# A two-layer graph network on one core: the sums of a group of edges scattered one group behind the gathers' turn instead of two

## The chip, the cores and the metric

The kernel runs on 1 core of one Trainium2 chip. What is measured is the device time of one execution in microseconds; the kernel before takes 5044.54 us, the median of 3 runs (5033.79 to 5050.71).

## The reference

A graph of 50,000 nodes with 256 features and 50,000 edges, sorted by `dst`, goes through two layers, each with a residual and a layer norm:

```
x = layernorm(x + GAT(x, src, dst, edge_attr_32))       # attention, 4 heads of 64
h = concat(x[src], x[dst])                              # 50000 x 512
h = tanh(h @ W0 + b0); h = tanh(h @ W1 + b1); h = h @ W2 + b2
h = h * (edge_attr_128 @ Wg)
out = layernorm(x + segment_mean(h, src, n))
```

Everything is float32. The change is in the second layer, the edge network: for each edge, two rows of a table are gathered and added, a small network runs on them, and the result is added to the row of `out` that `src` names.

## The kernel before, in words

The kernel is a row of stages, each a block in which all engines run their own program. The edge network is the block that begins at L1493; the stage before it has already written, for each node, the rows of two tables in the chip's memory: PA (the part of `x @ W0` for one end of an edge, with the reciprocal of the node's number of edges in column F0) and PB (that for the other end), and has put `x` into `out`. The stage after it reads `out` and normalizes it.

**Tiling.** Edges are worked on in 98 groups (`GROUPS`) of 4 tiles (`G`) of 128 edges. Buffers are double, by the parity `s` of the group `g`; a "turn" is one pass of each engine's `body(g, ...)`. `late(g, n)` and `early(g, n)` leave work out in the last and first n turns. There is no planner: each engine's order is written out by hand, and semaphores tie the engines together. `need(engine, sem, n)` is a wait, left out if n is not positive.

**GpSimd** issues all indirect DMAs of the stage, strictly in its order. `gather(s, j)` (L1508 to L1513) issues two, a tile's rows of PA into `u_pa` and of PB into `u_pb`; the two have one line, L1510. `free(g)` waits until the buffers of a group may be written: the adds of the group two before it (`v_sum`) and its transposes (`p_t`) must be done. `scatter(g, s, j)` (L1521 to L1531, DMA at L1528) adds the 128 rows of sums of tile j from `u_sums` to the rows of `out` named in `u_row`. It waits for ScalarE's copy of the sums (`a_y`, one copy for j = 0, 1 and one for j = 2, 3), for VectorE's row numbers (`v_si`), and for j = 0 and 2 until all scatters issued before have landed (`o_st`). Before the loop, groups 0 and 1 are gathered. In turn g GpSimd calls `free(g + 2)`, then gathers tiles 0, 1 of group g + 2, scatters two tiles, gathers tiles 2, 3, scatters two tiles (L1538 to L1547).

**VectorE** in turn g selects for group g - 1 (`select`: which edges have the same `src`), computes its row numbers (`scatter_rows`, L1805), subtracts for the low parts of layers 1 and 2 (`low0(g + 1)`, `low1(g)`), multiplies by the gate (`message(g, j)`, L1810), and late in the turn adds the gathered rows of group g + 2: `add_first` (L1747), which waits until all eight gathers of the group have landed, then `message(g, 3)`, then `add_rest`. The order there is message 2, low part of 1, add_first, message 3, low parts of 2 and 3, add_rest; the select of group g follows at the start of the next turn.

**TensorE** in turn g: layer 1 of group g in three parts (nine products at L1580 and one at L1594 each), between which stand the transposes of group g + 1 (L1568, part k needs the k-th add); then `combine(g - 1, 0)` (L1620, adds up messages with the same `src` within a tile or a pair of tiles), the gate and layer 2 of group g, with the transposes of edge features and `combine(g - 1, 1)` between.

**ScalarE** does the tanh's in the same order, and `sums(g - 1, 0)` and `sums(g - 1, 1)` (L1696), which copy the combined messages of group g - 1 to `u_sums` in turn g. The first waits until the scatters of group g - 3 have landed.

**SP** loads edge features and keys, and waits for transposes and selections only.

Of the kernel before, what the change touches and what calls it, by code (L numbers as in the profile page):

```python
# [22 lines left out]
G = 4  # L23
# [33 lines left out]
def gnn_kernel(nc, x, src, dst, e128, e32, lin_W, att_src, att_dst, lin_edge_W, att_edge, bias,  # L57
# [7 lines left out]
    GROUPS = N // (G * P) + 1  # L65
# [36 lines left out]
    def groups(eng, body):  # L102


        for g in range(GROUPS):
            body(g, g % 2, g // 2, g == GROUPS - 1)
# [17 lines left out]
    def need(eng, sem, n):  # L124

        if not (isinstance(n, int) and n <= 0):
            eng.wait_ge(sem, n)

    def early(g, n):

        return isinstance(g, int) and g < n

    def late(g, n):

        return isinstance(g, int) and g + n >= GROUPS
# [11 lines left out]
    with top:  # L147
# [1314 lines left out]
        with ph:  # L1462
# [26 lines left out]
                                                        sem("u_msg_low"), sem("u_selected"), sem("u_scatter_rows"))  # L1489
            TB, LB, QB, CB = (B[0], B[1]), (B[2], B[3], B[4]), (B[5], B[6]), B[7]  # L1490
            NK = [n for _, n in M0[:3]] + [T0]

            with nc.Block() as block:  # L1493
# [12 lines left out]
                @block.gpsimd  # L1506
                def _(pool):
                    def gather(s, j):  # L1508
                        for q, (buf, table, w) in enumerate(((pa, PA, AW), (pb, PB, F0))):
                            pool.indirect_dma_start(  # L1510
                                out=buf[s][:, j, 0:w], out_offset=None, in_=table,
                                in_offset=bass.IndirectOffsetOnAxis(ap=ix[s][:, 1 - q, j:j + 1], axis=0))\
                                .then_inc(gath[s], 16)  # L1513

                    def free(g):
                        pool.wait_ge(v_ix, g + 1)
                        need(pool, v_sum, 4 * (g - 1))
                        need(pool, p_t, 4 * (g - 1))
                        pool.sem_inc(turn, 1)

                    def scatter(g, s, j):  # L1521

                        pool.wait_ge(a_y, 2 * g + j // 2 + 1)
                        pool.wait_ge(v_si, g + 1)
                        if j % 2 == 0:
                            need(pool, o_st, 16 * (4 * g + j))
                        pool.sem_inc(turn, 1)
                        pool.indirect_dma_start(  # L1528
                            out=out, out_offset=bass.IndirectOffsetOnAxis(ap=si[s][:, j:j + 1], axis=0),
                            in_=yo[s][:, j, :], in_offset=None, bounds_check=N - 1, oob_is_err=False,  # L1530
                            compute_op=ALU.add).then_inc(o_st, 16)  # L1531

                    for g in range(2):
                        free(g)
                        for j in range(G):
                            gather(g, j)

                    def body(g, s, i, last):  # L1538
                        if not late(g, 2):
                            free(g + 2)  # L1540
                        for h in range(G // 2):
                            for j in (2 * h, 2 * h + 1):
                                if not late(g, 2):
                                    gather(s, j)
                            for j in (2 * h, 2 * h + 1):
                                if not early(g, 2):
                                    scatter(g - 2, s, j)  # L1547
                    groups(pool, body)
                    for g in range(GROUPS - 2, GROUPS):
                        for j in range(G):  # L1550
                            scatter(g, g % 2, j)
                    pool.wait_ge(o_st, 16 * G * GROUPS)

                @block.tensor
                def _(pe):
# [45 lines left out]
                    def layer2(g, s, j):  # L1601
                        e = slice(j * P, (j + 1) * P)
                        for k, (_, n) in enumerate(M1):
                            n += k == 2
                            if j == 0:
                                pe.wait_ge(v_hm, 3 * g + k + 1)
                            o = product(QB[j % 2][:, 0:D], [h2[q][0:n, k, e] for q in range(2)],
                                        [w2r[q][0:n, k, :] for q in range(2)], k == 0, k == 2)
                        o.then_inc(p_q, 1)
# [368 lines left out]
```

## Time and profile before

| | |
|---|---|
| median of the runs | 5044.54 us |
| span of the profiled execution | 5498.8 us |
| edge network in it, first gather to last scatter | 3303.8 to 5183.7 us |
| TensorE matmul busy, whole span | 4252.2 us, 77% |
| VectorE, ScalarE, GpSimd busy | 3806.6, 3248.7, 3300.0 us |
| indirect DMAs of the edge network | 784 gathers, 392 scatters |

The runs were timed without the profiler, and the times in the rows are of another execution, with it. Of that one only the span, from its first to its last instruction, is given and no time of its own on the runs' scale; it is 454 us longer than the median. Times in rows are microseconds from the span's start. On GpSimd a DMA's duration is what the engine spends on issuing it, not the transfer. A matmul's end is modelled, and some records can be missing.

### The profile page before, as it was taken

The numbers are of one execution on the slowest core, as the hardware profiler recorded it, in microseconds if no ns is written. First come the engines' busy times: TensorE is split into PE (matmuls) and PEld (weight loads), VectorE is DVE, ScalarE is ACT, GpSimd is POOL, SyncE is SP. The second block draws the span as 40 slices with busy tenths as digits, with TensorE's granted clock in tenths as the row PEclk, the third lists the DMA queues.
The fourth block names the chain that finished last, engine by engine and source line by source line (L and its number), as shares of the span: only waits on it lengthen the run. The fifth ranks groups of instructions, "written<-read, shape, count | busy, mean of one in ns | idle before, by whom it ended". The sixth has DMA issues, their size and how long they took to land. (4 is left out here: it accounts for less than half of the span.)

```text
span 5498.8 us, 87081 instructions
## 1 busy us (share of the span) xinstructions
PE 4252.2 (77%) x24476; PEld 3420.0 (62%) x24476; DVE 3806.6 (69%) x12195; ACT 3248.7 (59%) x7255; POOL 3300.0 (60%) x3036
## 2 busy tenths in 40 slices
PE   6777777777657776599999997889989999999500
PEld 3455545555434444599999995777777777777400
DVE  7766666666656665798989875666666666666564
ACT  7755555555533343366666665666666676666575
POOL 0255555555666665455555546777777888888532
PEclk9999999999977887799999998999999999999755
DMA  3232322323275555699999995666666666666596
GB/s 82 55 86 80 87 80 81 88 80 84 71 150 166 166 165 166 221 368 354 367 353 365 355 322 139 143 141 145 144 150 139 146 149 148 147 151 145 144 394 275
DMA packets 774331, 975.10 MB, mean 177 GB/s; under 512 B 182069, under 2 KB 685148, under 8 KB 761084
## 3 DMA queue, kind: packets, MB, share of 16 engines
q0 software_dynamic: 170176, 323.19, 26.3%
q10 hardware_dynamic: 269085, 374.19, 18.9%
q1 hardware_dynamic: 334715, 273.49, 16.5%
q8 instruction: 162, 2.65, 0.2%
q14 instruction: 193, 1.58, 0.1%
HBM read 541.99 MB, written 429.16 MB: 177 GB/s over the span
## 5 line engine op out<-in xcount | busy, mean ns | idle before, releaser
L1381 PE MATMUL bank<-w0r,n_x1T 128*128 128x406 f32 x4704 | 905.8, 352 | 36.1 <-issue 16.9
L1381 PEld LDWEIGHTS bank<-w0r,n_x1T 128*128 128x128 f32 x4704 | 870.4, 190 | 59.9 <-ACT n_pa L1429 35.3
L1528 POOL DMA_INDIRECT out_x<-u_sums,u_row x392 | 639.5, 1631 | 143.8 <-issue 116.8
L580 POOL DMA_INDIRECT DS<-by_dst,rank_int x392 | 376.0, 959 | 572.8 <-DVE rank_int L750 427.8
L1580 PE MATMUL bank<-u_h,w1r 128*108 128x512 f32 (+1 forms) x2646 | 680.0, 401 | 0.0
L406 PEld LDWEIGHTS bank<-wst,xT 128*128 128x128 f32 x2352 | 332.2, 201 | 430.1 <-issue 311.4
L406 PE MATMUL bank<-wst,xT 128*128 128x264 f32 x2352 | 409.5, 312 | 242.6 <-DVE xps L415 196.8
L832 POOL DMA_INDIRECT xg<-XP,m_src x392 | 420.3, 1072 | 222.7 <-DVE msg L892 113.5
L1257 POOL DMA_INDIRECT n_cg<-CT,n_last x392 | 445.8, 1137 | 175.3 <-issue 95.2
L1510 POOL DMA_INDIRECT u_pa<-PA,u_rows x392 | 408.5, 1042 | 202.1 <-issue 111.1
L1580 PEld LDWEIGHTS bank<-u_h,w1r 128*108 128x108 f32 (+1 forms) x2646 | 436.6, 172 | 127.1
L1580 PE MATMUL bank<-w2r,u_h 108*128 108x256 f32 x3528 | 486.0, 282 | 7.0 <-DVE u_h L1775 6.9
L586 POOL DMA_INDIRECT DS<-r_s_dst,r_head_rows x392 | 387.9, 990 | 142.1 <-issue 117.3
L1510 POOL DMA_INDIRECT u_pb<-PB,u_rows x392 | 396.8, 1012 | 120.6 <-issue 117.9
L1684 ACT ACTIVATE u_gate<-bank,u_rc 128x256 f32<-128x256 f32 x392 | 186.6, 476 | 462.0 <-PE bank L1580 251.8
L1580 PEld LDWEIGHTS bank<-w2r,u_h 108*128 108x128 f32 x3528 | 448.6, 190 | 9.1 <-DVE u_h L1775 8.5
L1810 DVE TENSOR_TENSOR u_message<-bank,u_gate 128x256 f32<-128x256 f32 x392 | 166.1, 424 | 382.6 <-ACT u_gate L1684 262.0
L663 PE MATMUL bank<-table,ohloT 128*128 128x392 f32 x784 | 349.4, 529 | 44.5 <-ACT ohloT L603 43.5
L1568 PE MATMUL bank<-ident,u_pb 128*128 128x128 f32 (+1 forms) x1568 | 246.3, 280 | 157.6 <-DVE u_pb L1747 60.5
L1568 PEld LDWEIGHTS bank<-ident,u_pb 128*128 128x128 f32 (+1 forms) x1568 | 172.8, 137 | 266.9 <-issue 163.9
L718 DVE CUSTOM_DVE_ANT_0 found<-bank,onehot,earlier 128x392 f32<-128x392 f32 x392 | 243.0, 620 | 132.9 <-PE bank L663 58.7
L415 DVE TENSOR_TENSOR xps<-bank,biasx 128x264 f32<-128x264 f32 x392 | 166.0, 423 | 242.9 <-remote 232.7
(286 smaller groups left out, 10637.8 us busy)
## 6 DMA issues: line engine op xcount, KB each, us to landing
PA<-n_pa ACTq DMA_DIRECT2D x98, 816.0 KB
PB<-n_pb ACTq DMA_DIRECT2D x98, 812.0 KB
XP<-xps ACTq DMA_DIRECT2D x98, 528.0 KB
CT<-ct ACTq DMA_DIRECT2D x98, 528.0 KB
n_xp<-XP SPq DMA_DIRECT2D x98, 528.0 KB
xin<-in_x SPq DMA_DIRECT2D x97, 512.0 KB
n_x<-in_x SPq DMA_DIRECT2D x97, 512.0 KB
out_x<-n_x ACTq DMA_DIRECT2D x97, 512.0 KB, 4.8
```

The lines of the kernel that those rows point to most:

```text
L406: o = nc.tensor.matmul(acc[:, 0:XW], xT[k][p][:, h, j * P:(j + 1) * P], wst[q][:, h, :], start=(n == 0), stop=(n == 5))
L580: pool.indirect_dma_start(out=DS, out_offset=bass.IndirectOffsetOnAxis(ap=ri[s][:, j:j + 1], axis=0), in_=pd[s][:, j, :], in_offset=None). ...
L586: pool.indirect_dma_start(out=DS, out_offset=bass.IndirectOffsetOnAxis(ap=hx[s][:, j:j + 1], axis=0), element_offset=8, in_=sn[s][:, j, :] ...
L663: nc.tensor.matmul(UB[j % 2][:, 0:NT], oT[s][:, j * P:(j + 1) * P], tab[s][:], start=True, stop=True)\
L718: nc.vector.tensor_tensor_reduce(out=lkj[j % 2][:], in0=UB[j % 2][:, 0:NT], in1=ohhi[0][s][:, j, :], scale=1.0, scalar=cnt[s][:, j:j + 1], ...
L832: pool.indirect_dma_start(out=xg[r][:, j, :], out_offset=None, in_=XP, in_offset=bass.IndirectOffsetOnAxis(ap=sr[r][:, j:j + 1], axis=0))\
L1257: pool.indirect_dma_start(out=cg[s][:, j, :], out_offset=None, in_=CT, in_offset=bass.IndirectOffsetOnAxis(ap=il[s][:, j:j + 1], axis=0)). ...
L1381: o = nc.tensor.matmul(acc, xT[s][p][:, k, e], w0r[q][:, 2 * half + k, :], start=(n == 0), stop=(n == len(terms) - 1))
L1510: pool.indirect_dma_start(out=buf[s][:, j, 0:w], out_offset=None, in_=table, in_offset=bass.IndirectOffsetOnAxis(ap=ix[s][:, 1 - q, j:j + ...
L1528: pool.indirect_dma_start(out=out, out_offset=bass.IndirectOffsetOnAxis(ap=si[s][:, j:j + 1], axis=0), in_=yo[s][:, j, :], in_offset=None, ...
L1568: o = nc.tensor.transpose(TB[k % 2][0:n, j * P:(j + 1) * P], pb[s][:, j, a:a + n], ident[:])
L1580: o = nc.tensor.matmul(acc, a[p], b[q], start=(start and n == 0), stop=(stop and n == 2))
```

## The change

In GpSimd's loop, the scatters of turn g are those of group g - 1, whose parity is 1 - s, instead of those of group g - 2. They start in turn 1 instead of turn 2, and behind the loop one group is left to scatter instead of two. The other engines' programs are the same, and so are the numbers of DMAs and their sizes.

```diff
                             for j in (2 * h, 2 * h + 1):
-                                if not early(g, 2):
-                                    scatter(g - 2, s, j)
+                                if not early(g, 1):
+                                    scatter(g - 1, 1 - s, j)
                     groups(pool, body)
-                    for g in range(GROUPS - 2, GROUPS):
-                        for j in range(G):
-                            scatter(g, g % 2, j)
+                    for j in range(G):
+                        scatter(GROUPS - 1, 1, j)
                     pool.wait_ge(o_st, 16 * G * GROUPS)
```

## Rows read from the trace of the kernel before

**Rows 1.** Costliest groups of the page: busy us, mean ns | idle before, its main releaser.
```profile
L1528 POOL DMA_INDIRECT out_x<-u_sums,u_row x392 | 639.5, 1631 | 143.8 <-issue 116.8
```
**Rows 2.** Windows, turns 2 to 96: length, busy time of each engine, clock, DMA.
```profile
core 0: us, PE busy (x) PEld busy (x) DVE busy (x) ACT busy (x) POOL busy (x), PEclk, DMA share, GB/s
3374.28:5135.69 1761.41, 1606.02 (x10342) 1346.51 (x10340) 1158.91 (x3107) 1201.90 (x2353) 1384.76 (x1124) 0.99 0.66 145
```
**Rows 3.** Timeline, TensorE (start, length): marks of turns 2, 49 and 96.
```profile
3374.28 0.40 PE L1594 MATMUL bank<-u_h1t,w1t 86*108 86x512 f32 x1
...
4268.95 0.40 PE L1594 MATMUL bank<-u_h1t,w1t 86*108 86x512 f32 x1
...
5135.69 0.40 PE L1594 MATMUL bank<-u_h1t,w1t 86*108 86x512 f32 x1
```
**Rows 4.** Waits of GpSimd, edge network: total us, times, longest.
```profile
POOL u_pa L1510 <- PE bank L1568: 57.0, 23, 10.0
...
POOL out_x L1528 <- DMA out_x<-u_sums,u_row: 23.5, 7, 4.2
...
POOL out_x L1528 <- ACT u_sums L1696: 3.2, 1, 3.2
```
**Rows 5.** Timeline, GpSimd, one turn: first gather, second scatter pair, next turn's gathers.
```profile
4501.74 1.02 POOL L1510 DMA_INDIRECT u_pa<-PA,u_rows  x1 [0.32 <-issue]
...
4516.46 1.62 POOL L1528 DMA_INDIRECT out_x<-u_sums,u_row  x1 [0.30 <-issue]
...
4520.28 1.02 POOL L1510 DMA_INDIRECT u_pa<-PA,u_rows  x1 [0.31 <-issue]
...
4524.14 0.95 POOL L1510 DMA_INDIRECT u_pb<-PB,u_rows  x1 [0.30 <-issue]
```
**Rows 6.** Timeline, ScalarE, same turn: copies of the sums.
```profile
4500.23 0.68 ACT L1696 COPY u_sums<-bank 128x512 f32<-128x512 f32 x1
...
4504.07 0.58 ACT L1696 COPY u_sums<-bank 128x512 f32<-128x512 f32 x1
...
4517.82 0.68 ACT L1696 COPY u_sums<-bank 128x512 f32<-128x512 f32 x1
```
**Rows 7.** Timeline, VectorE, same turn: first add, then message 3.
```profile
4506.49 0.68 DVE L1747 TENSOR_TENSOR u_pb<-u_pb,u_pa 128x512 f32<-128x512 f32 x1
4510.20 0.42 DVE L1810 TENSOR_TENSOR u_message<-bank,u_gate 128x256 f32<-128x256 f32 x1 [3.03 <-ACT u_gate L1684]
```
**Rows 8.** Timeline, TensorE, same turn: transposes and layer 1.
```profile
4508.66 0.60 PE L1568 MATMUL bank<-ident,u_pb 128*128 128x128 f32 x4
...
4509.02 2.33 PE L1580 MATMUL bank<-u_h,w1r 128*108 128x512 f32 x9
...
4512.19 0.66 PE L1568 MATMUL bank<-ident,u_pb 128*128 128x128 f32 x4 [0.60 <-DVE u_pb L1747]
```
**Rows 9.** Timeline, start of the stage: eighth gather, VectorE's first add.
```profile
3312.69 0.95 POOL L1510 DMA_INDIRECT u_pb<-PB,u_rows  x1 [0.30 <-issue]
...
3315.93 1.89 DVE L1747 TENSOR_TENSOR u_pb<-u_pb,u_pa 128x512 f32<-128x512 f32 x3 [10.74 <-DMA u_pb<-PB,u_rows]
```
**Rows 10.** Timeline, end of the stage: sums of group 96, scatters.
```profile
5158.32 0.60 ACT L1696 COPY u_sums<-bank 128x512 f32<-128x512 f32 x1
...
5160.36 1.55 POOL L1528 DMA_INDIRECT out_x<-u_sums,u_row  x1 [3.22 <-DMA out_x<-u_sums,u_row]
...
5182.10 1.55 POOL L1528 DMA_INDIRECT out_x<-u_sums,u_row  x1 [0.30 <-issue]
```
**Rows 11.** Windows: turn 5, and a part of it.
```profile
3430.34:3451.73 21.39, 18.68 (x112) 15.93 (x113) 13.37 (x36) 13.73 (x28) 16.33 (x15) 0.92 0.67 138
...
3442.50:3445.80 3.30, 3.01 (x14) 3.04 (x15) 1.85 (x4) 2.00 (x4) 2.39 (x4) 0.50 0.59 170
```
**Rows 12.** Timeline, TensorE: two waits, and matmuls behind the first.
```profile
3358.68 0.66 PE L1568 MATMUL bank<-ident,u_pb 128*128 128x128 f32 x4 [2.40 <-DVE u_pb L1747]
...
3359.10 2.34 PE L1580 MATMUL bank<-u_h,w1r 128*107 128x512 f32 x9
...
3441.55 0.62 PE L1580 MATMUL bank<-w2r,u_h 108*128 108x256 f32 x3 [1.28 <-DVE u_h L1775]
```

## The prediction

> **What bounds the kernel now.** I read the page first for where GpSimd stands, then the windows of the edge network, then single turns of its loop. A turn is the time in which the kernel's bodies work on one group of 512 edges; there are 98. The change touches only GpSimd's order of indirect DMAs in this stage.
>
> One row has all the full turns: from turn 2 to turn 96, TensorE is busy 1606 of 1761 us (91%) and GpSimd 1385 (79%), at a granted clock of 0.99 [rows 2]. The last layer-1 matmul of a turn's first third marks its start; by the first and last of these marks 94 turns take 1761.41 us, 18.74 each; from turn 49 on 47 turns take 866.74 us, 18.44 each [rows 3].
>
> GpSimd is fuller than 79%. In one turn its first gather starts at 4501.74 and that of the next turn at 4520.28: 18.54 us, filled by 8 gathers and 4 scatters with 0.30 us before each [rows 5]. Its real waits in the whole stage are 57.0 us for transposes (23 times), and 3.2 us once for the sums that a scatter reads [rows 4]. So GpSimd and TensorE both need about 18.4 us a turn, and GpSimd stays in step because what it does in a turn was ready long before: the gathers run two groups ahead, the scatters take sums made one turn earlier.
>
> **The change, part by part.** In turn g GpSimd issues: gathers j=0,1 of group g+2; two scatters; gathers j=2,3; two scatters. Number, order and size of the DMAs stay. The four scatters are now those of group g-1, not g-2. What is removed is a turn of slack; what is added is that the first pair waits for ScalarE's first copy of the sums of g-1, which is made in this same turn.
>
> Queued behind that wait are the four gathers j=2,3 of group g+2 and the other pair. VectorE's first add of g+2 wants all eight gathers and stands in VectorE's queue before message(g,3), so the late gathers hold VectorE, then TensorE (the transposes of g+2 after its first third of layer 1, and the combination of group g), and so the next copy of sums. It is a closed loop of one turn:
>
> 1. Copy done, GpSimd sees it: 0.30 us, the idle that stands before each of its DMAs [rows 5].
> 2. Two scatters and four gathers: from 4516.46 to 4524.14 + 0.95 = 4525.09, so 8.63 us [rows 5].
> 3. From the last gather's end on GpSimd to its landing. At the start of the stage the eighth gather ends at 3312.69 + 0.95 = 3313.64 and VectorE, waiting for it, starts at 3315.93: 2.29 us [rows 9]. It is an almost empty queue there, so this is a lower end; I take 2.3 and allow 3.
> 4. The first add: 0.68 us [rows 7].
> 5. From there to the next copy's end. VectorE starts message(g,3) at 4510.20 and the copy ends at 4517.82 + 0.68 = 4518.50: 8.30 us, the lower end [rows 6, 7]. By TensorE: transposes 0.60, layer 1's second third from 4509.02 to the next transposes at 4512.19, less their wait of 0.60, 2.57 us, then from 4512.19 to 4518.50, 6.31 us: with 0.1 of hand-over 9.6 us, the upper end [rows 6, 8]. I take 9.0, since the two chains cross: ScalarE's activations need TensorE's products and the reverse.
>
> Sum: 0.30 + 8.63 + 2.3 + 0.68 + 9.0 = 20.9 us (20.2 to 22.2), against 18.74 now. GpSimd's own work of 18.5 fits inside it.
>
> The check from the other side: today message(g,3) starts 4510.20 - 4500.91 = 9.29 us after the copy ended [rows 6, 7]. After the change the gathers land 11.2 us after it and the add ends at 11.9. That is 2.6 us late, and what fills the 9.29 us today (the rest of layer 2, the next layer 1) can all be done within the 11.9. This turn, 9.29 + 8.30 = 17.6 us, is shorter than the mean; on the mean, 2.6 us more would be 21.3, between the ends.
>
> The second pair of scatters costs nothing: the second copy starts 3.84 us after the first, while GpSimd still has 8.63 us to do [rows 5, 6]. Nor does the wait of each pair for the landing of the pair before: four gathers lie between, as now. SP's loads are tied to transposes and selections, not to scatters.
>
> **The clock.** TensorE will have a gap of 2 to 3 us in each turn, between its layer-1 third and the late transposes. In the trace such a gap is at times followed by the lower level, 1.2 GHz: behind a 1.28 us wait at 3441.55 the clock reads 0.50 for 3442.50 to 3445.80, and that turn took 21.39 us at a mean of 0.92 [rows 11, 12]. But behind the gap of 2.40 us at 3358.68 nine layer-1 matmuls took 2.34 us, as long as the 2.33 of nine at 4509.02 [rows 8, 12]. Lost by such an episode is 8% of 21.39, 1.7 us of matmuls, and it would lie on the path, just behind the gap. I take one turn in two: 0.85, so 21.7 us. The Trainium skill ("TensorE: Matmul & The Clock Gate", Part 1: The HAM clock gate) says that the clock is binary, half rate as the default after idleness and full rate only after sustained work. By that rule each turn could pay, and the sum would be 22.6 us a turn and not 21.7; the rows so far show both outcomes.
>
> **Ends.** Turns 1 to 95 have gathers behind the wait: 95 turns. At the end, the sums of group 96 are ready at 5158.92; today's last four pairs start at 5160.36, some 6.6 us apart, because each waits for the pair before to land, and end at 5183.65. With the change four pairs are left too, of groups 96 and 97, and the first starts at 5159.2: 1.1 us gained [rows 10].
>
> Total: 95 x (21.7 - 18.74) = 281, less 1: +280 us. The profiled execution spans 5498.8 us, so its successor about 5779. That span is 454 us above the median of 5044.5 of the runs timed; the page doesn't say where. I carry the difference over as it is, 5325, or in proportion (5.1%), 5301, and say 5320.
>
> **The rivals.**
> - *The clock falls in every turn.* 20.9 + 1.7 = 22.6 us, 95 x 3.86 = 367, so 5410. For it: the gap is there in every turn. Against: the 2.40 us gap. Chance 0.18.
> - *The runs without a profile have a shorter loop.* If the 454 us lie in the 2352 indirect DMAs (six groups of 392 on the page; one is in [rows 1]), each is 0.19 us shorter, the six in the loop 1.2 us. With the clock's share it is 20.5 against 18.74: +170, so 5215. Chance 0.15.
> - *No change.* The loop is shorter than a turn of today, so the wait costs nothing. All of 20.9 - 18.7 = 2.2 us would have to go, 0.37 us of each of the six DMAs, over a third of a gather's 0.95. Chance 0.04.
> - *Faster.* Turns 2 to 48, in which GpSimd is early and waits for transposes, take 894.67 us, 19.04 each; from 49 on, where it runs later, 18.44 [rows 3, 4]. If its early gathers disturb TensorE's feeders, tying GpSimd to this turn's sums gives all turns the later phase: 47 x 0.60 = 28 us, so 5016. The point from which this decides is whether the gathers land before their add is due: it must start 9.29 - 0.68 = 8.6 us after the copy, and they land at 11.2. 2.6 us are missing, each turn. Chance 0.04.
> - *The scatters don't really move*, because something else holds them. Their rows (v_si) and sums are made in the turn in which they now stand, and the landing of the previous pair came in time in all but 7 cases, 23.5 us [rows 4]. I see nothing that could; it has no chance of its own.
>
> **How the numbers follow.** The forecast, 5320, has 0.59; its own range is 5230 (20.9 us a turn and no clock loss gives 205 us, so 5249, or 188 less in proportion, 5232) to 5400. The range of 8 in 10 goes from 5190, which takes in most of the shorter loop, to 5430. A measurement of this kernel can tell about 0.3% (15 us) from no change. Slower by more: 0.59 + 0.18 + 0.15 = 0.92; within: 0.04; faster: 0.04.
>
> **What would show it in the profile after.** GpSimd's busy time stays near 3300 us, but before the scatters there is idle time ended by ScalarE's copy of the sums, about 3 us in each of some 95 turns, 250 to 350 us, where it is 3.2 now [rows 4]. The last gather of a turn ends some 9 us behind the copy. VectorE waits before the first add for the landing of the gathers, 4 to 6 us a turn, and TensorE before the transposes of L1568 for VectorE, 2 to 3 us a turn. The marks stand 21 to 22.5 us apart. The clock in the edge network shows dips beside 0.99: in half of the turns if I am right on that term.
>
> I am wrong if the marks stay within 19 us (then the gathers weren't late, or VectorE's add had more slack than 9.29 us shows), or if GpSimd's wait for the sums is long but VectorE's for the gathers is not.

## The result, and the profile after

The kernel after takes 5597.91 us (median of 4 runs, 5593.02 to 5601.06) beside 5039.16 us for the kernel before: 1.1096 times as long, 95% interval 1.1078 to 1.1115. Run again, on a chip where the kernel before takes 5049.11 us, it takes 5605.28 us, 1.1103 (1.1086 to 1.1120). I had forecast 5320 us: the right side and the right mechanism, but 280 us of a loss of 559, and 5598 lies outside my range of 8 in 10 (5190 to 5430).

A chip turned up later on which the kernel before takes 5525 us, where the others take some 5040 to 5050. Two other kernels were profiled on it, and they reach the first gather of the edge network at 3324 and 3348 us; the first profile of the kernel before (5498.8 us) reaches it at 3304, every other profile at 2917 to 2936. So the first profile most likely comes from a chip of that slower kind; which one it was isn't recorded, and the kernel before was not profiled there again. A second profile of the unchanged kernel, which spans 5051.9 us, is therefore what the kernel after is compared with here.

The page of the kernel after, in the columns of [rows 1]; the lines are those of L1528 and L1747, now L1746.

```profile
L1528 POOL DMA_INDIRECT out_x<-u_sums,u_row x392 | 645.1, 1646 | 706.9 <-ACT u_sums L1695 604.7
...
L1746 DVE TENSOR_TENSOR u_pb<-u_pb,u_pa 128x512 f32<-128x512 f32 x294 | 198.7, 703 | 617.3 <-DMA u_pb<-PB,u_rows 617.3
```

GpSimd's busy time is as before, but ahead of the scatters it now waits 604.7 us for ScalarE's copy of the sums, where [rows 4] had 3.2; VectorE waits 617.3 us for gathers, 6.3 us a turn.

The marks of turns 2 and 96 as in [rows 3], then windows as in [rows 2] of the same 94 turns, of three parts of turn 62, and of the whole stretch in it at the lower level, before and behind the start of its transposes:

```profile
2984.80 0.40 PE L1593 MATMUL bank<-u_h1t,w1t 86*108 86x512 f32 x1
...
5227.77 0.40 PE L1593 MATMUL bank<-u_h1t,w1t 86*108 86x512 f32 x1
```

```profile
core 0: us, PE busy (x) PEld busy (x) DVE busy (x) ACT busy (x) POOL busy (x), PEclk, DMA share, GB/s
2984.80:5227.77 2242.97, 1808.05 (x10341) 1519.58 (x10340) 1176.34 (x3101) 1201.46 (x2350) 1352.18 (x1129) 0.86 0.52 115
4413.00:4419.00 6.00, 2.79 (x15) 1.85 (x13) 0.37 (x2) 0.77 (x2) 4.78 (x5) 1.00 0.65 156
4419.50:4426.00 6.50, 5.53 (x16) 4.16 (x17) 6.21 (x20) 2.81 (x6) 5.09 (x5) 0.50 0.65 111
4426.50:4431.80 5.30, 5.30 (x38) 4.62 (x37) 2.59 (x5) 4.65 (x10) 0.00 (x0) 1.00 0.48 163
...
4419.41:4420.47 1.06, 0.00 (x0) 0.00 (x0) 0.82 (x2) 0.00 (x0) 0.78 (x1) 0.50 0.57 48
4420.47:4426.24 5.77, 5.77 (x17) 4.40 (x18) 5.59 (x20) 3.05 (x6) 4.55 (x5) 0.50 0.64 119
```

A turn takes 2242.97 / 94 = 23.86 us. The clock is 0.86 in the mean, because within each of the 94 turns it reads 1.00, then 0.50, then 1.00 again; in this one it is at 0.50 for 6.83 us, from 4419.41 to 4426.24. Here is that turn's loop, from one copy of sums to the next; it answers to [rows 5 to 8]. Timeline of the kernel after, by engine:

```profile
4407.29 0.62 ACT L1695 COPY u_sums<-bank 128x512 f32<-128x512 f32 x1
...
4431.23 0.62 ACT L1695 COPY u_sums<-bank 128x512 f32<-128x512 f32 x1
```

```profile
4408.84 1.62 POOL L1528 DMA_INDIRECT out_x<-u_sums,u_row  x1 [5.83 <-ACT u_sums L1695]
...
4412.65 1.02 POOL L1510 DMA_INDIRECT u_pa<-PA,u_rows  x1 [0.30 <-issue]
...
4416.51 0.95 POOL L1510 DMA_INDIRECT u_pb<-PB,u_rows  x1 [0.30 <-issue]
...
4432.78 1.62 POOL L1528 DMA_INDIRECT out_x<-u_sums,u_row  x1 [6.41 <-ACT u_sums L1695]
```

```profile
4419.65 0.77 DVE L1746 TENSOR_TENSOR u_pb<-u_pb,u_pa 128x512 f32<-128x512 f32 x1 [6.28 <-DMA u_pb<-PB,u_rows]
4420.34 0.41 DVE L1809 TENSOR_TENSOR u_message<-bank,u_gate 128x256 f32<-128x256 f32 x1
```

```profile
4415.40 0.40 PE L1593 MATMUL bank<-u_h1t,w1t 86*108 86x512 f32 x1
...
4420.47 1.11 PE L1567 MATMUL bank<-ident,u_pb 128*128 128x128 f32 x4 [4.68 <-DVE u_pb L1746]
...
4421.24 4.19 PE L1579 MATMUL bank<-u_h,w1r 128*108 128x512 f32 x9
```

The copy ends at 4407.91; the scatter starts at 4408.84, the last gather ends at 4417.46, the add starts at 4419.65, and the next copy ends at 4431.85. TensorE has been idle for 4.68 us when the transposes come, and the nine layer-1 matmuls behind them take 4.19 us where nine took 2.33 in [rows 8]: the clock granted to them is the lower level, 1.2 GHz.

The same rows of the kernel before in its second profile: the windows of turns 2 to 96, and one turn.

```profile
2997.95:4682.31 1684.36, 1570.78 (x10341) 1338.41 (x10340) 1160.48 (x3097) 1201.86 (x2349) 1342.67 (x1122) 0.99 0.70 152
```

```profile
3846.50 1.02 POOL L1510 DMA_INDIRECT u_pa<-PA,u_rows  x1 [0.30 <-issue]
...
3864.34 1.02 POOL L1510 DMA_INDIRECT u_pa<-PA,u_rows  x1 [0.31 <-issue]
```

```profile
3853.53 0.74 DVE L1747 TENSOR_TENSOR u_pb<-u_pb,u_pa 128x512 f32<-128x512 f32 x1 [2.59 <-DMA u_pb<-PB,u_rows]
...
3854.32 0.66 PE L1568 MATMUL bank<-ident,u_pb 128*128 128x128 f32 x4 [0.94 <-DVE u_pb L1747]
```

A turn takes 1684.36 / 94 = 17.92 us there, not 18.74. GpSimd has no idle time but its 0.3 us, and VectorE already waits 2.59 us for its gathers: GpSimd bounds the kernel before on these chips. The difference of 5.94 us over 95 turns is 564 us, beside the measured 559.

### The profile page after: what moved, and what is told of

It is laid out like the page before. It is cut to its first block and busy times, and to the rows that moved or that the text cites. A ratio compares the mean times of both kernels' runs of the same rounds, so it can differ in the third digit from the quotient of the medians.

```text
span 5595.5 us, 87081 instructions
## 1 busy us (share of the span) xinstructions
PE 4335.8 (77%) x24476; PEld 3537.5 (63%) x24476; DVE 3832.6 (68%) x12195; ACT 3247.0 (58%) x7255; POOL 3263.0 (58%) x3036
## 5 line engine op out<-in xcount | busy, mean ns | idle before, releaser
L1528 POOL DMA_INDIRECT out_x<-u_sums,u_row x392 | 645.1, 1646 | 706.9 <-ACT u_sums L1695 604.7
L1579 PE MATMUL bank<-u_h,w1r 128*108 128x512 f32 (+1 forms) x2646 | 854.8, 479 | 0.0
L1567 PE MATMUL bank<-ident,u_pb 128*128 128x128 f32 (+1 forms) x1568 | 311.5, 335 | 471.8 <-DVE u_pb L1746 461.3
L1579 PEld LDWEIGHTS bank<-u_h,w1r 128*108 128x108 f32 (+1 forms) x2646 | 543.3, 213 | 172.2
L1746 DVE TENSOR_TENSOR u_pb<-u_pb,u_pa 128x512 f32<-128x512 f32 x294 | 198.7, 703 | 617.3 <-DMA u_pb<-PB,u_rows 617.3
L1567 PEld LDWEIGHTS bank<-ident,u_pb 128*128 128x128 f32 (+1 forms) x1568 | 244.6, 174 | 562.7 <-DVE u_pb L1746 483.3
L1689 ACT CAST u_msg<-u_message 128x256 fp32r<-128x256 f32 x392 | 158.4, 404 | 614.3 <-DVE u_message L1809 614.3
L406 PE MATMUL bank<-wst,xT 128*128 128x264 f32 x2352 | 384.1, 299 | 116.8 <-DVE xps L415 111.8
L1672 ACT ACTIVATE u_h<-bank,b1s 108x512 fp32r<-108x512 f32 (+1 forms) x294 | 201.9, 687 | 293.4 <-PE bank L1593 293.4
L1774 DVE TENSOR_TENSOR u_h<-bank,u_h 108x512 fp32r<-108x512 f32 (+1 forms) x294 | 202.4, 688 | 198.0 <-ACT bank L1673 198.0
L663 PE MATMUL bank<-table,ohloT 128*128 128x392 f32 x784 | 322.6, 493 | 0.0
```

The source lines that it names most:

```text
L406: o = nc.tensor.matmul(acc[:, 0:XW], xT[k][p][:, h, j * P:(j + 1) * P], wst[q][:, h, :], start=(n == 0), stop=(n == 5))
L663: nc.tensor.matmul(UB[j % 2][:, 0:NT], oT[s][:, j * P:(j + 1) * P], tab[s][:], start=True, stop=True)\
L1528: pool.indirect_dma_start(out=out, out_offset=bass.IndirectOffsetOnAxis(ap=si[s][:, j:j + 1], axis=0), in_=yo[s][:, j, :], in_offset=None, ...
L1567: o = nc.tensor.transpose(TB[k % 2][0:n, j * P:(j + 1) * P], pb[s][:, j, a:a + n], ident[:])
L1579: o = nc.tensor.matmul(acc, a[p], b[q], start=(start and n == 0), stop=(stop and n == 2))
L1774: nc.vector.tensor_tensor(h2[1][0:n, m, :], LB[m][0:n, :], h2[0][0:n, m, :].bitcast(f32), ALU.subtract).then_inc(v_hm, 1)
```

## The experiments

Each was timed beside the kernel before on the same chip; `turn` is the mean of turns 2 to 96 in its profile.

| kernel | us | beside before | ratio (95%) | turn | clock |
|---|---|---|---|---|---|
| before again | 5050.35 | 5050.35 | 0.9997 (0.9985 to 1.0009) | 17.92 | 0.99 |
| after | 5597.91 | 5039.16 | 1.1096 (1.1078 to 1.1115) | 23.86 | 0.86 |
| after, filled | 5371.80 | 5050.35 | 1.0639 (1.0618 to 1.0660) | 21.26 | 1.00 |
| one slot | 5051.39 | 5050.35 | 0.9999 (0.9986 to 1.0012) | 17.98 | 1.00 |
| three and one | 5230.31 | 5050.35 | 1.0353 (1.0332 to 1.0374) | 19.96 | 0.93 |
| three and one, filled | 5124.61 | 5048.27 | 1.0147 (1.0128 to 1.0165) | 18.87 | 1.00 |
| four first | 5325.73 | 5048.27 | 1.0549 (1.0531 to 1.0567) | 20.91 | 0.91 |
| before, three scatters | 4887.25 | 5048.27 | 0.9681 (0.9665 to 0.9698) | 16.39 | 1.00 |
| after, add later | 5603.33 | 5048.27 | 1.1096 (1.1073 to 1.1119) | 23.89 | 0.86 |
| one and three, other chip | 6185.92 | 5524.98 | 1.1205 (1.1140 to 1.1270) | 25.63 | 0.83 |
| before, filled, other chip | 5555.50 | 5524.98 | 1.0058 (1.0024 to 1.0091) | 19.30 | 0.98 |
| before, filled | 5056.25 | 5049.11 | 1.0014 (1.0005 to 1.0023) | 18.01 | 1.00 |

**The kernel before again.**

> The kernel before, unchanged, for a second profile of it. The first profile spans 5498.8 us where its timed runs take 5039, the profile of the kernel after 5595.5 where they take 5598. If the first profile was an unusual execution, this one spans about 5040 us, its edge network has turns of about 18.0 us (5598 - 5039 = 559 us over 95 turns is 5.9, and the changed kernel's turns are 23.89), and the stages before the edge network are as long as in the changed kernel (2920 us to its first gather). If profiling lengthens this kernel alone, it spans about 5500 again. Time: same as before.

It spans 5051.9 us, so profiling does not lengthen this kernel: the profiled execution took 5053.66 us and the nine others 5038.5 to 5058.6. The rows above of the kernel before are from this run.

**The clock alone: the kernel after, with its gap filled.** Twelve matmuls, whose result the transposes overwrite.

```diff
+                    def fill(g, s, n):
+                        need(pe, v_e, g + 1)
+                        for _ in range(n):
+                            nc.tensor.matmul(TB[0][0:108, :], w1r[0][:, 0, 0:108],
+                                             h1[s][0][:, 0, :], start=True, stop=True)
...
                         layer1(g, s, 0)
                         if ahead:
+                            fill(g, s, 12)
                             transposes(g + 1, 1 - s, 0)
```

> The kernel after, with 12 extra 512-column matmuls of TensorE in each turn (their result is overwritten) in the gap before the transposes that wait for the late gathers. They need about 3 us and stand in a gap of 4.7 us. Theory A (a closed loop of 21 us a turn through the late gathers, and on top the clock, which falls in every turn behind the gap and costs 2 to 3 us): the clock of the edge network returns to 0.97 to 1.0, the turn shrinks from 23.9 to 21 to 21.5 us, the time to 5320 to 5380 us; the wait for the gathers stays. Theory B (the clock is a companion, the turn is set by GpSimd's and the DMA queue's order alone): the clock returns but the turn stays at 23.9 us or grows, 5600 us or more.

Windows of turns 2 to 96, and TensorE around the gap (the filler is L1573), in the filled kernel:

```profile
3007.62:5006.00 1998.38, 1823.37 (x11470) 1523.90 (x11468) 1158.36 (x3101) 1199.83 (x2350) 1343.60 (x1129) 1.00 0.60 129
```

```profile
4368.81 2.91 PE L1573 MATMUL bank<-u_h,w1r 128*108 128x512 f32 x12
4373.37 0.66 PE L1567 MATMUL bank<-ident,u_pb 128*128 128x128 f32 x4 [1.66 <-DVE u_pb L1752]
4373.78 2.33 PE L1584 MATMUL bank<-u_h,w1r 128*108 128x512 f32 x9
```

TensorE does 2.91 us more work a turn and still waits 1.66 us for the add, the nine matmuls are back at 2.33 us, and the turn is 2.60 us shorter. So the time splits as theory A has it: 21.26 us of loop, 2.60 us of clock. Theory B is out. The parts of the loop say where the 2.60 us lie. In the mean of 92 turns of the timelines, from the end of a copy to the end of the last gather it is 9.56 us in both kernels, from there to the end of the add 2.92 unfilled and 2.96 filled, and from the add to the end of the next copy 11.41 us unfilled and 8.74 filled. Only the last part, in which TensorE's chain runs, has changed.

**One slot earlier instead of two.** The loop, against the kernel before; behind it six tiles are left to scatter.

```diff
-                            for j in (2 * h, 2 * h + 1):
-                                if not early(g, 2):
-                                    scatter(g - 2, s, j)
+                            for j in (0, 1):
+                                if h == 0 and not early(g, 2):
+                                    scatter(g - 2, s, 2 + j)
+                                if h == 1 and not early(g, 1):
+                                    scatter(g - 1, 1 - s, j)
```

> Half of the change: the scatters come one pair of slots earlier than before, not two (in turn g first tiles 2, 3 of group g-2, then, behind all gathers of g+2, tiles 0, 1 of group g-1). GpSimd still waits for sums made in the same turn, but no gather of group g+2 stands behind that wait. Theory A: the loop is open, the gathers land some 15 us before they are due, turns of 18 us, 5040 us within 1%. Theory B' (waiting for sums of the same turn is what costs, whatever stands behind it): half or more of the loss, 5300 us or more.

No difference. It is a weaker test than I meant: GpSimd is late enough in these turns that it waited for the sums in only 2 places (11.3 us). What it shows is that a pair taken from the same turn's sums costs nothing in this place, where the sums are nearly always ready and no gather of g+2 stands behind it. What a real wait would cost there was not tested.

**Half of the gathers behind the wait.**

```diff
-                            for j in (2 * h, 2 * h + 1):
+                            for j in ((0, 1, 2), (3,))[h]:
                                 if not late(g, 2):
                                     gather(s, j)
```

> The kernel after, but three tiles of group g+2 are gathered before the first pair of scatters and one behind it, so two gather DMAs stand behind the wait and not four. Theory A: the loop is 2.5 us shorter (two issues of 1.25 us), 21.4 us a turn if the clock still falls in every turn, 18.5 to 19 if it doesn't: 5360 or 5080 to 5130 us, and VectorE's wait for the gathers shrinks by as much. Theory B' (it counts only whether GpSimd waits): 5600 us.

5230 us lies between the two figures of theory A, because the clock falls in some turns and not in others: 72 of the 94 turns are of 20.3 us and 22 of 18.8. In one of the shorter a wait of 1.83 us is followed by matmuls at full length; in one of the longer, which starts at 4108.85, the wait is 2.37 us, the nine matmuls take 3.86, and the clock of the window is 0.91:

```profile
3955.48 0.66 PE L1567 MATMUL bank<-ident,u_pb 128*128 128x128 f32 x4 [1.83 <-DVE u_pb L1746]
3955.89 2.35 PE L1579 MATMUL bank<-u_h,w1r 128*108 128x512 f32 x9
...
4111.62 0.66 PE L1567 MATMUL bank<-ident,u_pb 128*128 128x128 f32 x4 [2.37 <-DVE u_pb L1746]
4112.03 3.86 PE L1579 MATMUL bank<-u_h,w1r 128*108 128x512 f32 x9
```

```profile
4109.00:4128.00 19.00, 16.63 (x106) 14.24 (x105) 12.49 (x33) 12.53 (x25) 13.48 (x12) 0.91 0.61 133
```

The length of the wait alone doesn't sort the turns: the 72 in which the clock falls have waits of 1.75 to 2.81 us, the 22 others of 1.66 to 2.44.

**The same, filled** (`fill(g, s, 6)`, as above).

> Three tiles before the scatters and one behind, with 6 extra 512-column matmuls of TensorE a turn in the gap before the late transposes. Theory A: without them the turns are of 18.9 and 20.5 us, the longer with a fall of the clock (mean 19.96, clock 0.93); filled, the clock is 0.99 to 1.0 and the turn 18.7 to 19, 5110 to 5150 us. If the clock is not what makes the longer turns, 5230 us or more.

5125 us, a turn of 18.87 and a clock of 1.00: as theory A had it, and the clock's share in the unfilled one is 1.09 us. Without the clock, the two points of the loop are 21.26 us with four gather DMAs behind the wait and 18.87 with two, 2.39 us apart, where two issues of 1.25 are 2.50.

**All four tiles first.** `for j in ((0, 1, 2, 3), ())[h]:` in the same place.

> The kernel after, but all four tiles of group g+2 are gathered before the four scatters of group g-1: no gather of g+2 stands behind the wait any more. Theory A: the closed loop through the gathers is gone, but the second pair of scatters now waits for the landing of the first with nothing between them (about 3 us, as at the end of the stage), and GpSimd's own turn becomes 8 x 1.25 + 4 x 1.9 + 3 = 20.6 to 21 us, which then sets the turn: 5300 to 5340 us, with GpSimd's wait on the landing of scatters, not on ScalarE's sums. Rival (each wait for sums of the same turn costs as in the kernel after): 5600 us.

Its waits, in the columns of [rows 4], and its windows:

```profile
POOL out_x L1528 <- DMA out_x<-u_sums,u_row: 254.7, 79, 4.0
...
POOL out_x L1528 <- ACT u_sums L1695: 17.5, 3, 7.9
```

```profile
2992.54:4957.83 1965.29, 1700.72 (x10341) 1439.10 (x10340) 1171.16 (x3097) 1199.42 (x2349) 1333.57 (x1126) 0.91 0.59 131
```

The wait for the sums has gone (17.5 us), and GpSimd's own turn, which now contains the landing of the first pair, sets 20.91 us in the mean (TensorE's single turns range from 16.4 to 24.0). The closed loop is opened by moving gathers alone, and another bound stands behind it.

**What bounds the kernel before.** The scatter of tile 3 is left out in each group, and its counts in the waits with it.

```diff
-                                if not early(g, 2):
+                                if not early(g, 2) and j < 3:
                                     scatter(g - 2, s, j)
```

> The kernel before, with the scatter of every group's tile 3 left out, so its output lacks those sums. It tells what bounds the kernel before: theory A (its second profile has GpSimd filled to the last 0.3 us and VectorE waiting 2.6 us a turn for gathers): GpSimd is the bound, 1.9 us less of issue gives turns of 16.1 to 16.6 us, 4890 to 4930 us. Rival (TensorE bounds it at 18.4 us a turn, as I read the first profile): 5020 to 5050 us.

```profile
2981.99:4522.38 1540.39, 1540.39 (x10342) 1346.59 (x10340) 1172.82 (x3102) 1211.08 (x2350) 1212.32 (x1031) 1.00 0.67 158
```

One issue of 1.9 us less gives 1.53 us, and then TensorE is busy 1540.39 of 1540.39 us: its own need is 16.39 us a turn, and the kernel before is bound by GpSimd at 17.92. My reading of both at 18.4 us was of the other profile, and too high for TensorE even there: by [rows 2] it was busy 1606.02 / 94 = 17.1 us a turn.

**Which chain comes after the add.** VectorE's `add_first` of the kernel after is moved behind `message(g, s, 3)` and the two `low_message` calls.

> The kernel after, with VectorE's first add of group g+2 moved behind message(g,3) and the two low parts, so that these and ScalarE's work on them no longer wait for the gathers. Theory A1 (behind the add, TensorE's chain sets the next sums: transposes, two thirds of layer 1 at the low clock, combination): nothing or up to 0.3 us a turn gained, 5560 to 5610 us. Theory A2 (ScalarE's chain from message(g,3) on sets it, 8.3 us in the kernel before): 1 us and more a turn gained, 5500 us or less.

5603 us and 23.89 us a turn: nothing gained. ScalarE's chain, which begins with message 3, is not what sets the next copy; theory A1, TensorE's chain, holds.

**More gathers behind the wait.** `for j in ((0,), (1, 2, 3))[h]:` in the same place.

> The kernel after, with one tile of group g+2 gathered before the first pair of scatters and three behind it: six gather DMAs behind the wait and not four. Theory A (the loop is 0.3 + 3.8 + 1.25 x the gather DMAs behind the wait + landing + add + TensorE's chain, and the clock's share on top): 2.5 us a turn more than the 23.86 of the kernel after, 26.4 us, 5830 us within 30. If the longer gap lets the clock stay low for longer, up to 1.7 us more, 5990 us. Rival (the turn of the kernel after is one into which the loop just happens to lock): 5600 us, or no line through the three kernels.

It fell on the other kind of chip, so its 6186 us can't be put beside 5598, and I take only its turn, 25.63 us at a clock of 0.83: 1.77 us more than the kernel after, where I expected 2.5. The wait in front of TensorE's transposes grows from 4.6 to 7.2 us a turn. The parts of the loop tell where the missing 0.7 us are. In the mean of 92 turns, from the copy's end to the end of the last gather it is 12.08 us and not 9.56, 2.52 more for two DMAs; landing and add together are 2.94 us, as in the kernel after (2.92); and from the add to the next copy it is 10.59 us and not 11.41. One turn shows why:

```profile
4652.69 1.12 PE L1567 MATMUL bank<-ident,u_pb 128*128 128x128 f32 x4 [7.16 <-DVE u_pb L1746]
4653.45 3.31 PE L1579 MATMUL bank<-u_h,w1r 128*108 128x512 f32 x9
```

```profile
4648.75:4652.70 3.95, 0.01 (x1) 0.02 (x1) 0.79 (x2) 0.00 (x0) 3.34 (x3) 0.50 0.57 121
4652.70:4655.58 2.88, 2.88 (x9) 2.37 (x10) 2.74 (x8) 2.58 (x5) 2.27 (x3) 0.50 0.66 83
```

More of the stretch at the lower level now falls into the gap, where TensorE has nothing to do. In the mean of the turns 4.5 us of it lie in the gap and 4.0 behind it, where the kernel after has 1.1 and 5.7. The loop without the clock grew as theory A has it, and the clock's share shrank. I have no run of the kernel after on that chip, so that its last part without the clock is 8.74 us there too is not shown.

**A version that might beat both.** The kernel before with `fill(g, s, 3)`, to take away the five turns of 20 us that its second profile has.

> The kernel before with 3 extra 512-column matmuls of TensorE a turn ahead of the transposes, in its gap of 0.9 us. Its second profile has 17.9 us turns set by GpSimd, but one in some twenty takes 20 us, with a dip of the clock (0.99 in the mean). If the dips make these turns, they go: 5 turns of 2.3 us, 10 to 12 us gained, 5036 to 5042 us beside 5050, faster than both kernels by 0.2%. If GpSimd alone sets the time and the dips are a companion: no change. If the matmuls get into TensorE's path: 5 to 50 us slower.

> The kernel before with the 3 extra matmuls again. It ran on the chip on which the kernel before takes 5525 us and TensorE has no gap for them: 0.6% slower. On a chip on which the kernel before takes 5045: 5033 to 5039 us if the dips of the clock make its turns of 20 us, 5045 if not. On the other kind of chip: 5550 again.

It doesn't: 0.6% slower on the other chip and 0.14% slower on the usual one. On the usual one the fill did what it should (no turn is longer than 19.2 us, where five were of 20.0 to 20.3, and the clock is 1.00), but the mean turn is 18.01 us, not below 17.92. GpSimd sets the mean: each of the five long turns was followed by one of 16.4 or 16.5 us, so what TensorE lost was made up in the next. On the other chip the clock still fell in 21 of the 94 turns, fill or not.

```profile
2998.01:4691.34 1693.33, 1628.58 (x10624) 1381.82 (x10622) 1159.17 (x3097) 1201.84 (x2349) 1351.77 (x1122) 1.00 0.69 151
```

**The kernel after again.**

> The kernel after, unchanged. One chip ran the kernel before in 5525 us where the others took 5040 to 5050, and its profile there has the turns of the first profile of the kernel before (18.7 us and more, GpSimd early, TensorE late). If this run falls on such a chip: theory A has the closed loop of the kernel after contain little of what is slower there, so a turn of 23.9 us again and a loss of 95 x (23.9 - 18.9) = 475 us, a ratio of about 1.085 and not 1.11. If it falls on a chip of the other kind: 5598 us and a ratio of 1.11, as before.

It fell on a chip of the usual kind and repeated the first result: 5605 us, GpSimd waiting 612.4 us for sums. The loss on the other kind of chip was not measured.

## Why the prediction was right in kind and half in size

**The mechanism: right.** The loop that the prediction describes is the one in the trace, step by step, and each of its joints answered to an experiment: fewer gathers behind the wait, a shorter turn (three and one); none, and the wait is gone (four first); the next sums set by TensorE's chain and not ScalarE's (add later).

**The sum was 280 us where 559 were lost. Three terms, of very different weight:**

- *The clock, the step that failed.* I took 1.7 us in one turn of two, 0.85 us. It fell in every turn and cost 2.60 us (filled or not, 23.86 - 21.26): 95 x 1.75 = 166 us. Two readings were at fault. First, I had TensorE's gap at 2 to 3 us, and it is 4.68. I had taken the 2.6 us by which the add comes too late for VectorE's message 3, but TensorE is ready for its transposes earlier than that. In [rows 8] they start at 4508.66, 7.75 us after the copy's end at 4500.91; in the kernel after the matmul ahead of them ends 7.89 us after the copy (4407.91 to 4415.80), the same. With my own 11.9 us for the add, the rows gave a gap of some 4 us. Second, the price of a fall, 1.7 us, came from a turn in which the clock reads 0.50 for 3.3 us [rows 11]. In the kernel after it reads so for 6.83 us, of which 1.06 lie in the gap and cost nothing; half of the 5.77 behind it, 2.9 us, is an estimate of the loss, and 2.60 are what the fill gives back. My rival "the clock falls in every turn" had the right case, but 1.7 of the 2.60 us and the turn of the other profile: 5410, not 5598.
- *The turn before.* 18.74 us in the profile I read, 17.92 on the chips that were timed: 95 x 0.82 = 78 us. I had seen that the span was 454 us longer than the runs, but used it only for a shorter loop, which no run shows (its DMAs take 8.62 us, I had 8.63); that the turn of before might be shorter too, which works the other way, I didn't price.
- *The loop without the clock.* 20.9 forecast, 21.26 measured: 34 us. In parts: from the copy's end to the first scatter 0.93 us and not 0.30 (4407.91 to 4408.84), since 0.30 is the idle between DMAs that wait for nothing; two scatters and four gathers 8.62 (forecast 8.63); landing 2.19 (2.3); the add 0.77 (0.68); from there to the next copy 8.74 in the filled kernel (9.0, which I had picked between two ends and not worked out).

Together 278 us, and 280 + 278 = 558. That the sum closes is arithmetic, since the terms are the differences of two sums; what supports each is the run that it was read from.

**The other steps.** The second pair of scatters and its landing cost nothing, as forecast. The last gather ends 9.55 us behind the copy, forecast some 9. The rest of the signs that I had named fell outside their bounds, by the errors above: GpSimd's wait for sums 604.7 us (250 to 350), VectorE's for gathers 6.3 us a turn (4 to 6), TensorE's 4.7 (2 to 3), marks at 23.86 (21 to 22.5). The rival "faster" rested on turns of 19.04 and 18.44 us, where the usual chips have 17.92, and "no change" needed a loop under 17.9.

**On the rule.** The windows of turn 62 show a clock of 1.00, then 0.50 from 4419.41, when TensorE has been idle since 4415.80, and 1.00 again 6.83 us later; each of the 94 turns has such a fall. The two levels and the fall after idleness that the Trainium skill ("TensorE: Matmul & The Clock Gate", Part 1: The HAM clock gate) describes are what the trace shows. The same section of the Trainium skill puts the ramp at the start of work at under 1% of a typical kernel's span, and it also describes, as oscillation, a loop that waits for a DMA in each pass and pays the transition each time. This case is of the second sort: 95 x 2.60 = 247 us, 4.4% of 5598. The times of the two kernels differ by less, 226 us, since in its profile the filled one starts turn 2 later by 22.8 us.

## What to carry to other kernels

Ask of a moved wait not only how long it lasts but whether what is queued behind it feeds the very thing it waits for: if so, the turn becomes the length of that loop, and each microsecond on it is paid in full every turn, a fallen clock for as long as it outlasts the gap. Measure a new gap from where TensorE itself stands ready, and not from another engine's lateness. Price it with the clock fallen until a run shows otherwise, and fill it to tell the two shares apart. If the profiled execution is much longer than the timed runs, it may be of another chip: work out the turn before for both, since that shifts one end of the difference and perhaps not the other.

## What I had not expected of the hardware

- Chips differ: the same kernel takes some 5040 to 5050 us on three and 5525 us on a fourth, of which the first stages alone are a large part (first gather of the edge network at 2920 us in the kernel after, 3324 and 3348 us in the two profiles of that chip). Its cause wasn't looked for, nor whether it is the chip or its condition at the time. GpSimd's DMAs, their landing and the add take the same time in the loop of one and three, which ran there.
- A gather's landing took 2.19 us (2.2 in the mean of the turns) behind the last of a row of DMAs in the loaded loop, and 2.29 us at the start of the stage [rows 9]: the load of the queues didn't show in it.
- Filling a gap of TensorE with matmuls whose results are thrown away made the kernel after 226 us faster (5597.9 to 5371.8), with 12 matmuls more a turn.
